# Turning half of x2 on VectorE and by transfers instead of TensorE, in a fused attention and feed-forward kernel

## The chip, the cores and the metric

The kernel runs on one core of one Trainium2 chip. The metric is device time in microseconds (us). A profile of one execution stands beside the times.

## What is computed

Inputs are x (32 batches, 32 steps, 512 features, float32), a condition index and a length per batch, and the weights of one layer. Cut to what matters:

```python
h = einsum('bct,bcd->bdt', x, cond_w[cond_idx])        # mix of the 32 steps, per batch
q, k = rms_norm(h @ Wq + bq, gq), rms_norm(h @ Wk + bk, gk)   # 4096 wide
v = h @ Wv + bv                                        # 32 heads of 128
x2 = x + softmax(q k^T / sqrt(128)) v @ Wo + bo
K = kernel(log_dt, C, log_A_real, A_imag, 512)         # 32 channels, 512 taps
y = causal_conv(x2, K) + x2 * D                        # along the 512 features
y = y * (arange(512) < length[batch])
out = x2 + y @ ffn_w + ffn_b + lora(y, gate, lora_a, lora_b) + shared_lora(y)
```

The step axis of x2 (32) is the channel axis of the convolution, and its feature axis (512) is the time along which the convolution runs.

## The kernel before

All engines have an instruction stream written out by hand, with semaphores between them. Tokens are (batch, step) pairs, 1024 of them, in G = 8 groups of P = 128 tokens: group g holds batches 4g to 4g + 3 (BPG = 4), each with 32 steps. Features are cut into KC = 4 chunks of 128. TensorE's products are split in three (high times high, high times low, low times high), so one product of 128 contraction rows is three matmuls.

The stages, in order: the mix; q, k and the scores for 32 heads; the values; then eight attention units (UNITS), each of one group of eight heads (OCT) and one half of the tokens (HG = 4 groups). A unit n has attend(n), 64 matmuls into the banks of PV_BANK; ACT's attn_out(n), which evicts them into at_hi; DVE's, which makes at_lo; then project_first(n) and project_second(n, g), which multiply by Wo into O_BANK; and DVE's accumulate(n, ...), which adds each of the four groups to acc. acc starts as x + bo and is x2 at the end. Unit 6 is the last for groups 0 to 3, unit 7 for groups 4 to 7. acc_ok counts DVE's additions.

The convolution wants x2 with the features on the partitions. So transpose_x2(g) (L1113) turns one group on PE, four transposes of 128x128 into a bank, and ACT's x2_out(g) (L1481) evicts the bank into x2p, laid out [feature, step, chunk, batch]. In unit 7, groups 0 to 3 are turned between project_first and project_second, groups 4 and 5 between the projections, and 6 and 7 after them. Then come five small matmuls (spin, L1165), whose result isn't used, and convolve(0). convolve(u) (L1137) does four channels, one in each 32-column quadrant of PE: for each chunk, x2p as the stationary operand (32 batches) and a Toeplitz view of the kernel (toep0 for u < 4, toep1 then) as the moving one. DVE masks the result (y_tok), PE turns it back (turn), ACT writes y_hi and y_t, DVE y_lo. The low-rank products and the feed-forward follow, and DVE adds acc to each group of the output (L1923).

DMA: SP's queue issues nearly all transfers in one order. In unit 7 these are ffn_raw (L450), toep0 (L453, 4 MB), sixteen small transfers of a_turn (L456) and four of b_turn (L458) to DRAM, all in pieces of 128 B, and, once these have landed, a_all, b_all and fb_rows. a_turn and b_turn are the low-rank weights turned by DVE in 32x32 blocks (L1877, L1878). POOL adds the feed-forward's bias (fb_rows) to acc, group by group (L795), and DVE waits for that before it adds acc to the output. ACT's own queue is used only for a few small loads at the start.

The addresses of several tiles overlap in time: x2p has the place of p_blocks, the attention weights of the unit being computed.

## Time and profile before

| | us |
|---|---|
| three runs | 806.17, 805.47, 806.24 |
| median | 806.17 |
| the profiled execution | 805.49 |
| its span in the profile | 803.7 |

The granted TensorE clock is 1.0 in the whole span. Busy shares of the span: PE 99%, PE's weight loads 81%, DVE 80%, POOL 65%, ACT 41%. The page also gives the chain of waits that ended last, the costliest groups of instructions and the transfers. All moments below are in us from the start of the span.

### The profile page before, as it was taken

The numbers are of one execution on the slowest core, as the hardware profiler recorded it, in microseconds if no ns is written. First come the engines' busy times: TensorE is split into PE (matmuls) and PEld (weight loads), VectorE is DVE, ScalarE is ACT, GpSimd is POOL, SyncE is SP. The second block draws the span as 40 slices with busy tenths as digits, with TensorE's granted clock in tenths as the row PEclk, the third lists the DMA queues.
The fourth block names the chain that finished last, engine by engine and source line by source line (L and its number), as shares of the span: only waits on it lengthen the run. The fifth ranks groups of instructions, "written<-read, shape, count | busy, mean of one in ns | idle before, by whom it ended". The sixth has DMA issues, their size and how long they took to land.

```text
span 803.7 us, 15196 instructions
## 1 busy us (share of the span) xinstructions
PE 795.6 (99%) x6093; PEld 651.7 (81%) x6093; DVE 643.1 (80%) x646; ACT 332.2 (41%) x374; POOL 520.5 (65%) x451
## 2 busy tenths in 40 slices
PE   9999999999999999999999999999999999999998
PEld 7777888888888888888888888888888888888466
DVE  7799888888888888987889769989899888861442
ACT  4655555555555555572222226322422331322520
POOL 4999887333333333428998995979999999910420
PEclk9999999999999999999999999999999999999999
DMA  7031111111111111304434421456404813418502
GB/s 207 28 85 50 52 52 52 53 52 52 52 52 52 52 52 42 115 2 157 182 139 180 180 105 55 169 79 187 157 1 157 316 61 147 157 50 257 127 18 88
DMA packets 80735, 81.87 MB, mean 102 GB/s; under 512 B 26044, under 2 KB 61212, under 8 KB 78652
## 3 DMA queue, kind: packets, MB, share of 16 engines
q1 hardware_dynamic: 80188, 81.24, 31.2%
q8 instruction: 25, 0.41, 0.2%
q10 hardware_dynamic: 512, 0.13, 0.1%
q14 instruction: 10, 0.08, 0.0%
HBM read 64.97 MB, written 16.40 MB: 101 GB/s over the span
## 4 chain that ended last, share of the span: by engine, by line
PE 91%; DVE 3%; POOL 3%; ACT 2%; DMA 1%; issue 1%; SPq 0%; DVEq 0%; POOLq 0%
PE psum L862 13%; PE psum L864 12%; PE psum L863 12%; PE psum L808 7%; PE psum L810 7%; PE psum L809 7%; PE psum L1061 7%; PE psum L1090 4%; PE psum L1092 4%; PE psum L1091 4%; PE psum L1078 3%; PE psum L1080 3%; PE psum L1079 3%; PE psum L901 3%; PE psum L1149 1%; DMA w_raw<-in_wk 1%
## 5 line engine op out<-in xcount | busy, mean ns | idle before, releaser
L506 POOL TENSOR_TENSOR w_raw<-w_raw 128x256 f32<-128x256 f32 x31 | 45.1, 1454 | 123.1 <-DMA w_raw<-in_wk 122.6
L862 PE MATMUL psum<-t_hi,w_hi 128*128 128x512 f32 x248 | 100.5, 405 | 0.0
L864 PE MATMUL psum<-t_hi,w_lo 128*128 128x512 f32 x248 | 96.5, 389 | 0.0
L863 PE MATMUL psum<-t_lo,w_hi 128*128 128x512 f32 x248 | 96.5, 389 | 0.0
L1370 ACT ACTIVATE sq<-qk_sb 128x1024 f32<-128x1024 f32 x31 | 32.9, 1063 | 140.7 <-issue 127.5
L1637 DVE TENSOR_TENSOR sumsq<-sumsq,sq 128x1024 f32<-128x1024 f32 x62 | 80.2, 1295 | 0.0
L1409 ACT ACTIVATE at_hi<-psum,params 128x512 fp32r<-128x512 f32 x64 | 44.0, 688 | 69.6 <-PE psum L1061 69.6
L862 PE MATMUL psum<-mix_hi,w_hi 128*128 128x512 f32 x186 | 72.5, 390 | 0.2 <-DVE w_lo L1541 0.2
L863 PE MATMUL psum<-mix_lo,w_hi 128*128 128x512 f32 x186 | 72.4, 389 | 0.0
L864 PE MATMUL psum<-mix_hi,w_lo 128*128 128x512 f32 x186 | 72.4, 389 | 0.0
L1541 DVE TENSOR_TENSOR w_lo<-w_raw,w_hi 128x1792 fp32r<-128x1792 f32 x30 | 61.4, 2047 | 1.5 <-ACT w_hi L1246 1.5
L1061 PEld LDWEIGHTS psum<-p_blocks,v_sb 128*128 128x128 f32 x512 | 58.5, 192 | 0.7
L1061 PE MATMUL psum<-p_blocks,v_sb 128*128 128x128 f32 x512 | 58.6, 275 | 0.0
L1826 DVE SCALAR_TENSOR_TENSOR at_lo<-psum,params,at_hi 128x512 fp32r<-128x512 f32 x64 | 47.2, 748 | 11.4 <-ACT at_hi L1409 5.0
L862 PEld LDWEIGHTS psum<-t_hi,w_hi 128*128 128x128 f32 x248 | 46.5, 187 | 10.6 <-DVE qk_sb L1629 1.1
L864 PEld LDWEIGHTS psum<-t_hi,w_lo 128*128 128x128 f32 x248 | 46.5, 188 | 10.1
L863 PEld LDWEIGHTS psum<-t_lo,w_hi 128*128 128x128 f32 x248 | 46.6, 188 | 8.3
L1246 ACT ACTIVATE w_hi<-w_raw 128x1792 fp32r<-128x1792 f32 (+2 forms) x32 | 52.8, 1651 | 1.1 <-POOL w_raw L511 1.0
L1078 PE MATMUL psum<-wo_hi_a,at_hi 128*128 128x512 f32 x128 | 50.5, 395 | 1.0 <-DVE wo_lo_a L1796 1.0
L1090 PE MATMUL psum<-wo_hi_b,at_hi 128*128 128x512 f32 x128 | 50.3, 393 | 0.1
L1080 PE MATMUL psum<-wo_hi_a,at_lo 128*128 128x512 f32 x128 | 49.9, 389 | 0.0
L1092 PE MATMUL psum<-wo_hi_b,at_lo 128*128 128x512 f32 x128 | 49.8, 389 | 0.0
(287 smaller groups left out, 2130.2 us busy)
## 6 DMA issues: line engine op xcount, KB each, us to landing
v_sb<-v_scr_dram SPq DMA_DIRECT2D x6, 2048.0 KB, 7.9
v_scr_dram<-v_sb SPq DMA_DIRECT2D x9, 1024.0 KB, 3.9
w_raw<-in_wq SPq DMA_DIRECT2D x32, 256.0 KB, 2.9
w_raw<-in_wk SPq DMA_DIRECT2D x32, 256.0 KB, 3.2
wv_raw<-in_wv SPq DMA_DIRECT2D x16, 512.0 KB, 4.4
toep<-kpad_dram SPq DMA_DIRECT2D x2, 4096.0 KB, 14.5
wo_raw_a<-in_wo SPq DMA_DIRECT2D x4, 1024.0 KB, 5.2
wo_raw_b<-in_wo SPq DMA_DIRECT2D x4, 1024.0 KB, 5.2
```

Source lines behind the costliest of these rows:

```text
L808: mm(out, lh, rh, start=(fresh and n == 0), stop=False)
L809: mm(out, lh, rl, start=False, stop=False)
L862: mm(bank(n), wh, hi[:, c, tok], start=(i == 0), stop=False)
L863: mm(bank(n), wh, lo[:, c, tok], start=False, stop=False)
L864: last = mm(bank(n), wl, hi[:, c, tok], start=False, stop=(i == 1))
L1061: last = mm(bank(PV_BANK[u % 4])[:, P * g:P * g + P], v_sb[:, part, g, cols], p_blocks[:, u, g, :], start=True, stop=True)
L1078: mm(bank(O_BANK[g]), at_hi[:, h, tok], wo_hi_a[:, h, :], start=(h == 0), stop=False)
L1080: last = mm(bank(O_BANK[g]), at_lo[:, h, tok], wo_hi_a[:, h, :], start=False, stop=False)
L1090: mm(bank(O_BANK[g]), at_hi[:, QUAD + h, tok], wo_hi_b[:, h, :], start=False, stop=False)
L1092: last = mm(bank(O_BANK[g]), at_lo[:, QUAD + h, tok], wo_hi_b[:, h, :], start=False, stop=(h == QUAD - 1))
L1541: v.tensor_tensor(w_lo[slot][:].rearrange("p b n -> p (b n)"), w_raw[slot][:, 1:8, :].rearrange("p b n -> p (b n)"), w_hi[slot][:].rearran ...
L1637: v.tensor_tensor(sumsq[:, m, :], sumsq[:, m, :], sq[:, m, :], ALU.add).then_inc(total, 1)
```

## The change

Four things are changed together.

1. The groups stand on the token axis in the order 0, 2, 4, 6, 1, 3, 5, 7 (GROUP_AT): position 0 to 3 hold the even groups, and are the half that unit 6 completes. The loads of x into x_nat and acc fetch the rows in that order, mix_w is indexed by it, and the output's addition looks the position up.
2. Positions 0 to 3 are no longer turned on PE. After a_turn and b_turn, DVE turns each of them in 32x32 blocks into x2_turn. ACT issues sixteen transfers, one for each quadrant of 32 partitions that the data leave and each that they reach, from x2_turn to x2p, and convolve(0) waits for all (x2_moved).
3. x2p is laid out [feature, chunk, group, batch in the group, step]. ACT's evictions write 128 elements in a row; the convolution's stationary operand takes every 32nd element.
4. The last group (position 7) is added, turned and evicted in two halves of 256 features, the second half through another bank. Two small matmuls stand before the convolution, not five.

x2_turn has the place of the tiles sm_s, turns and prod, whose last use is the softmax of unit 7. In the diff, declarations of semaphores and of tiles that only move are left out.

```diff
@@ -46,6 +46,7 @@
 O_BANK = (0, 1, 6, 7)
 OUT_BANK = (6, 7, 4, 5)
 GROUP_ORDER = (3, 0, 1, 2)
+GROUP_AT = (0, 2, 4, 6, 1, 3, 5, 7)
 UNITS = ((3, 1), (3, 0), (0, 0), (0, 1), (1, 0), (1, 1), (2, 0), (2, 1))
 HG = G // 2
 NCOND, NLORA, RANK = 16, 16, 32
@@ -148,12 +149,13 @@
             [("mix_f", [P, KC, TOK], F32)],
             [("wv_raw", [P, 4, 2, 512], F32)],
             [("p_blocks", [P, OCT, HG, P], F32)],
-            [("x2p", [P, SEQ, KC, BATCH], F32)])
-
-        (las_nat, las_t, lbs_nat, lbs_t, kzero), (sm_s, turns, prod), (y_tok, o_stage) = overlay(
+            [("x2p", [P, KC, G, BPG, SEQ], F32)])
+
+        (las_nat, las_t, lbs_nat, lbs_t, kzero), (sm_s, turns, prod), (x2_turn,), (y_tok, o_stage) = overlay(
             [("las_nat", [P, KC, 32], F32), ("las_t", [P, KC, RANK], F32),
              ("lbs_nat", [P, KC, RANK], F32), ("lbs_t", [P, KC, 32], F32), ("kzero", [32, P], F32)],
             [("sm_s", [P, OCT, HG, 32], F32), ("turns", [P, 16, 32], F32), ("prod", [P, 16, 32], F32)],
+            [("x2_turn", [P, KC, KC, HG, SEQ], F32)],
             [("y_tok", [P, 2, FEAT], F32), ("o_stage", [P, 2, FEAT], F32)])
         u_tab = prod
         k_sb = turns[:, 0:8, :]
@@ -312,7 +315,7 @@
         @block.sync
         def _(sp):
             def load_x(n):
-                sp.dma_start(x_nat[:, 2 * n:2 * n + 2, :], x_rows[:, 2 * n:2 * n + 2, :]).then_inc(x_in[n], 16)
+                sp.dma_start(x_nat[:, 2 * n:2 * n + 2, :], x_rows[:, GROUP_AT[2 * n]:GROUP_AT[2 * n] + 3:2, :]).then_inc(x_in[n], 16)
             for n in range(2):
                 sp.dma_start(cond_nat[NCOND * n:NCOND * n + NCOND], cond_w.rearrange("n c d -> n (c d)")).then_inc(cond_in, 16)
@@ -411,7 +414,7 @@
             sp.dma_start(bo_rows, every_partition(bo, FEAT)).then_inc(bo_in, 16)
             sp.wait_ge(vp_mm, 2 * 28)
             for half in (1, 0):
-                sp.dma_start(acc[:, HG * half:HG * half + HG, :], x_rows[:, HG * half:HG * half + HG, :]).then_inc(acc_in[half], 16)
+                sp.dma_start(acc[:, HG * half:HG * half + HG, :], x_rows[:, half:G:2, :]).then_inc(acc_in[half], 16)
             for done in (vq1_out, vq2_out, vk2_out):
@@ -791,7 +794,10 @@
             gp.tensor_scalar(mask[:], mask[:], len_col[:, 0:1], None, ALU.is_lt).then_inc(mask_ok, 1)
             pool.wait_ge(bias_in, 16)
             for g in range(G):
-                pool.wait_ge(xt_mm, g + 1)
+                if g < HG:
+                    pool.wait_ge(x2_turned, g + 1)
+                else:
+                    pool.wait_ge(xt_mm, g - 3 if g < 7 else 5)
                 gp.tensor_tensor(acc[:, g, :], acc[:, g, :], fb_rows[:], ALU.add).then_inc(bias_ok, 1)
@@ -837,7 +843,7 @@
                         pe.wait_ge(mixf_ok, 1)
                 for c in range(KC):
                     last = mm(bank(2 + n % 6)[:, P * c:P * c + P], x_nat[:, g, P * c:P * c + P],
-                              mix_w[:, g, :], start=True, stop=True)
+                              mix_w[:, GROUP_AT[g], :], start=True, stop=True)
                 last.then_inc(mix_mm, 1)
@@ -1110,28 +1116,31 @@
                     if n == 0 and g == 1:
                         kern()
-            def transpose_x2(g):
-
-                pe.wait_ge(acc_ok, HG * 6 + g + 1)
-                if g >= 4:
-                    pe.wait_ge(x2p_ok, g - 3)
-                for c in range(KC):
-                    last = nc.tensor.transpose(bank(PV_BANK[g % 4])[:, P * c:P * c + P], acc[:, g, P * c:P * c + P], ident[:, :])
+            def transpose_x2(g, part=range(KC), to=None):
+
+
+                for c in part:
+                    last = nc.tensor.transpose(bank(PV_BANK[g % 4] if to is None else to)[:, P * c:P * c + P], acc[:, g, P * c:P * c + P], ident[:, :])
                 last.then_inc(xt_mm, 1)
             attend(7)
             project_first(7)
             pe.wait_ge(alo_ok, OCT * 8)
-            for g in range(4):
-                transpose_x2(g)
             project_second(7, 0)
             project_second(7, 1)
+            pe.wait_ge(acc_ok, HG * 7 + 1)
             transpose_x2(4)
             project_second(7, 2)
+            pe.wait_ge(acc_ok, HG * 7 + 2)
             transpose_x2(5)
             project_second(7, 3)
+            pe.wait_ge(acc_ok, HG * 7 + 3)
             transpose_x2(6)
-            transpose_x2(7)
+            pe.wait_ge(acc_ok, HG * 7 + 4)
+            transpose_x2(7, range(0, 2))
+            pe.wait_ge(acc_ok, HG * 7 + 5)
+            pe.wait_ge(x2p_ok, 1)
+            transpose_x2(7, range(2, 4), PV_BANK[0])
             def convolve(u):
@@ -1146,7 +1155,7 @@
                 for c in range(KC):
                     for q in range(BPG):
                         ch = 4 * u + q
-                        last = mm(bank(2 + u % 2)[quadrant(q), P * c:FEAT], x2p[:, ch, c, :],
+                        last = mm(bank(2 + u % 2)[quadrant(q), P * c:FEAT], x2p[:, c, :, :, ch].rearrange("p g b -> p (g b)"),
                                   backwards(toep[:, ch % 16, P * c:FEAT]), start=(c == 0), stop=(c == KC - 1),
                                   tile_position=(0, 32 * q))
                 last.then_inc(conv_mm, 1)
@@ -1162,8 +1171,9 @@
                                                ident[:, :])
                 last.then_inc(turn_mm, 1)
-            spin(5, ident[:, :], 7)
-            pe.wait_ge(x2p_ok, G)
+            spin(2, ident[:, :], 7)
+            pe.wait_ge(x2_moved, 16 * BPG * KC)
+            pe.wait_ge(x2p_ok, HG + 1)
             convolve(0)
             for u in range(1, 8):
                 convolve(u)
@@ -1478,14 +1488,22 @@
                     exp_scores(n + 2)
-            def x2_out(g):
-
-                act.wait_ge(xt_mm, g + 1)
-                sc.activation(x2p[:, :, :, BPG * g:BPG * g + BPG].rearrange("p s c b -> p c b s"),
-                              bank(PV_BANK[g % 4]).rearrange("p (c b s) -> p c b s", c=KC, b=BPG), ACT.Copy).then_inc(x2p_ok, 1)
-
-            for g in range(G):
-                x2_out(g)
+            act.wait_ge(x2_turned, HG)
+            for b in range(BPG):
+                for k in range(KC):
+                    act.dma_start(x2p[quadrant(k)].rearrange("p c (g e) b s -> p e b (c g) s", e=2)[:, 0, b],
+                                  x2_turn[quadrant(b), k].rearrange("p c g s -> p (c g) s")).then_inc(x2_moved, 16)
+
+            def x2_out(n, g, part=slice(0, KC), at=None):
+
+                act.wait_ge(xt_mm, n)
+                sc.activation(x2p[:, part, GROUP_AT[g], :, :],
+                              bank(PV_BANK[g % 4] if at is None else at).rearrange("p (c b s) -> p c b s", c=KC, b=BPG)[:, part], ACT.Copy).then_inc(x2p_ok, 1)
+
+            for n in range(1, 4):
+                x2_out(n, n + 3)
+            x2_out(4, 7, slice(0, 2))
+            x2_out(5, 7, slice(2, 4), PV_BANK[0])
             act.wait_ge(ffn_in, 16)
             sc.activation(ffn_hi[:].rearrange("p c n -> p (c n)"), ffn_raw[:].rearrange("p c n -> p (c n)"),
                           ACT.Copy).then_inc(fhi_ok, 1)
@@ -1876,11 +1894,21 @@
                     dve.wait_ge(lora, 2 * (2 * NLORA - 1))
                     v.transpose(a_turn[:].rearrange("p g c r -> p (g c) r"), a_sum[:].rearrange("p g (c f) -> p (g c) f", f=32)).then_inc(turned, 1)
                     v.transpose(b_turn[:].rearrange("p g c o -> p (g c) o"), b_sum[:].rearrange("p g c r -> p (g c) r")).then_inc(turned, 1)
+                    dve.wait_ge(acc_ok, HG * 7)
+                    for g in range(HG):
+                        v.transpose(x2_turn[:, :, :, g, :].rearrange("p k c s -> p c k s"),
+                                    acc[:, g, :].rearrange("p (c k f) -> p c k f", c=KC, k=KC)).then_inc(x2_turned, 1)
                 accumulate(n, (0, 1))
                 if n % 2 == 1 and n < 7:
                     split_o(n // 2 + 1, 0)
-                accumulate(n, (2, 3))
-
+                accumulate(n, (2, 3) if n < 7 else (2,))
+
+            for half in range(2):
+                cols = slice(256 * half, 256 * half + 256)
+                if half == 0:
+                    dve.wait_ge(wo_mm, HG * 8)
+                    dve.wait_ge(acc_ok, HG * 6)
+                v.tensor_tensor(acc[:, 7, cols], bank(O_BANK[3])[:, cols], acc[:, 7, cols], ALU.add).then_inc(acc_ok, 1)
             dve.wait_ge(fhi_ok, 1)
             v.tensor_tensor(ffn_lo[:].rearrange("p c n -> p (c n)"), ffn_raw[:].rearrange("p c n -> p (c n)"),
@@ -1920,7 +1948,7 @@
                 dve.wait_ge(out_mm, g + 1)
                 if g >= 2:
                     dve.wait_ge(out_dma[g % 2], 16 * (g // 2))
-                v.tensor_tensor(o_stage[:, g % 2, :], bank(OUT_BANK[g % 4]), acc[:, g, :], ALU.add).then_inc(out_ok, 1)
+                v.tensor_tensor(o_stage[:, g % 2, :], bank(OUT_BANK[g % 4]), acc[:, GROUP_AT.index(g), :], ALU.add).then_inc(out_ok, 1)
 _INS = [("x", "x", (TOK, FEAT), F32), ("cond_idx", "itok_B_0_15", (BATCH,), I32),
```

What moves on PE: the end of attention and the start of the convolution. L1119 and, after, L1123 are the transposes of x2 (acc into a bank), L1090 to L1092 and L1096 to L1098 the last projections, L817 and L823 the spin, L1149 and L1158 the convolution. Before, between the two projections of unit 7:

```order
L1080 MATMUL psum<-wo_hi_a,at_lo 128x512
L1119 MATMUL psum<-ident,acc 128x128 [waits acc_ok,alo_ok]
L1119 MATMUL psum<-ident,acc 128x128 x3
L1119 MATMUL psum<-ident,acc 128x128 [waits acc_ok]
L1119 MATMUL psum<-ident,acc 128x128 x3
L1119 MATMUL psum<-ident,acc 128x128 [waits acc_ok]
L1119 MATMUL psum<-ident,acc 128x128 x3
L1119 MATMUL psum<-ident,acc 128x128 [waits acc_ok]
L1119 MATMUL psum<-ident,acc 128x128 x3
L1090 MATMUL psum<-wo_hi_b,at_hi 128x512 [waits alo_ok,wolo_ok]
```

These sixteen are gone after. The end of PE's part before, from the last projection on:

```order
L1092 MATMUL psum<-wo_hi_b,at_lo 128x512
L1119 MATMUL psum<-ident,acc 128x128 [waits x2p_ok,acc_ok]
L1119 MATMUL psum<-ident,acc 128x128 x3
L1119 MATMUL psum<-ident,acc 128x128 [waits x2p_ok,acc_ok]
L1119 MATMUL psum<-ident,acc 128x128 x3
L817 MATMUL psum<-ident 128x128 x5
L1149 MATMUL psum<-toep,x2p 32x512 [waits toep_in0,x2p_ok]
```

and the same place after:

```order
L1098 MATMUL psum<-wo_hi_b,at_lo 128x512
L1123 MATMUL psum<-ident,acc 128x128 [waits acc_ok]
L1123 MATMUL psum<-ident,acc 128x128 x3
L1123 MATMUL psum<-ident,acc 128x128 [waits acc_ok]
L1123 MATMUL psum<-ident,acc 128x128
L1123 MATMUL psum<-ident,acc 128x128 [waits x2p_ok,acc_ok]
L1123 MATMUL psum<-ident,acc 128x128
L823 MATMUL psum<-ident 128x128 x2
L1158 MATMUL psum<-toep,x2p 32x512 [waits toep_in0,x2p_ok,x2_moved]
```

The last group's transposes stand in two pairs with a wait each, and the convolution waits for the transfers too.

ACT after its last evictions of attention (L1409, after L1419), before:

```order
L1409 ACTIVATE at_hi<-psum,params 128x512 [waits pv_mm] x8
L1484 ACTIVATE x2p<-psum 128x4x4x32 [waits xt_mm] x8
L1490 ACTIVATE ffn_hi<-ffn_raw 128x2048 [waits ffn_in]
L1497 ACTIVATE y_hi<-psum 128x128x4 [waits turn_mm]
L1498 ACTIVATE y_t<-psum 128x128x4
```

and after (x_turn is x2_turn):

```order
L1419 ACTIVATE at_hi<-psum,params 128x512 [waits pv_mm] x8
L1494 DMA x2p<-x_turn 32x16x32 [waits x2_turned]
L1494 DMA x2p<-x_turn 32x16x32 x15
L1500 ACTIVATE x2p<-psum 128x4x128 [waits xt_mm] x3
L1500 ACTIVATE x2p<-psum 128x2x128 [waits xt_mm] x2
L1508 ACTIVATE ffn_hi<-ffn_raw 128x2048 [waits ffn_in]
```

Five evictions stand where there were eight, and sixteen issues ahead of them.

## Rows read from the trace of the kernel before

**Rows 1.** The page, chain that ended last, shares of the span by engine

```profile
PE 91%; DVE 3%; POOL 3%; ACT 2%; DMA 1%; issue 1%; SPq 0%; DVEq 0%; POOLq 0%
```

**Rows 2.** The chain in order of time: start us, us, what

```profile
730.12 1.75 PE psum L1119 x16
...
743.73 0.45 PE psum L1119 x4
744.20 2.07 ACT x2p L1484 x2
```

**Rows 3.** Timeline (start us, us, engine, line, operation [idle before]) and one line's durations (ns)

```profile
721.80 1.20 DVE L1878 STREAM_TRANSPOSE b_turn<-b_sum 128x1024 f32<-128x1024 f32 x1
734.64 0.69 DVE L1840 TENSOR_TENSOR acc<-psum,acc 128x512 f32<-128x512 f32 x1 [11.63 <-PE psum L1092]
...
746.33 4.51 PE L1149 MATMUL psum<-toep,x2p 128*32 128x512 f32 x64
...
L1484 ACT ACTIVATE x2p<-psum x8: 1062/1090/1130, 730.6 to 745.2; 128x512 f32<-128x512 f32 x8
```

**Rows 4.** One line's durations, ns min/median/max: ACT's mix_f from PSUM

```profile
L1255 ACT ACTIVATE mix_f<-psum x4: 597/598/598, 11.1 to 16.5; 128x512 f32<-128x512 f32 x4
```

**Rows 5.** SP's queue, 723 to 727 us, and a_turn's sixteen transfers

```profile
723.44 4.19 SPq L456 DMA_DIRECT2D a_scr_dram<-a_turn  x1
...
L456 SPq DMA_DIRECT2D a_scr_dram<-a_turn x16: 450/458/4189, 723.4 to 739.0; - x16
...
DMA to landing us min/median/max: 1.6/2.9/12.7
```

**Rows 6.** DMA traffic of 727 to 730, 730 to 735 and 735 to 737 us

```profile
DMA packets 582, 1.19 MB, mean 397 GB/s; under 512 B 0, under 2 KB 0, under 8 KB 582
...
DMA packets 950, 1.95 MB, mean 389 GB/s; under 512 B 0, under 2 KB 0, under 8 KB 950
...
GB/s 205 573 205 392 262 144 254 192 228 241 192 205 203 220 203 210 220 203 215 202 208 208 213 208 205 218 195 215 187 162 98 123 189 195 131 57 16 13 13 8
DMA packets 2506, 0.38 MB, mean 191 GB/s; under 512 B 2464, under 2 KB 2464, under 8 KB 2506
```

**Rows 7.** DMA traffic of 741 to 743 and 539 to 544 us; b_turn's issues

```profile
DMA packets 2091, 0.28 MB, mean 140 GB/s; under 512 B 2090, under 2 KB 2090, under 8 KB 2090
...
DMA packets 5611, 0.72 MB, mean 144 GB/s; under 512 B 5593, under 2 KB 5611, under 8 KB 5611
...
739.52 3.72 SPq L458 DMA_DIRECT2D b_scr_dram<-b_turn  x4
```

**Rows 8.** Transfers of ACT's queue at the start: KB each, us from issue to landing

```profile
cond_i<-in_cond_idx ACTq DMA_DIRECT2D x1, 2.0 KB, 2.1
...
prm_nat<-in_bv ACTq DMA_DIRECT2D x1, 16.0 KB, 5.6
```

**Rows 9.** b_all's transfers, and timeline of what waits for the loads

```profile
b_all<-b_scr_dram SPq DMA_DIRECT2D x2, 256.0 KB, 7.4
...
748.05 0.56 SPq L466 DMA_DIRECT2D b_all<-b_scr_dram  x1
...
761.26 1.91 ACT L1504 ACTIVATE b_hi<-b_all 128x2048 fp32r<-128x2048 f32 x1
...
756.67 12.01 POOL L795 TENSOR_TENSOR acc<-acc,fb_rows 128x512 f32<-128x512 f32 x8 [10.62 <-DMA fb_rows<-in_ffn_b]
```

**Rows 10.** Weight loads, ns min/median/max, and busy us of each engine in one stretch

```profile
L1101 PEld LDWEIGHTS psum<-expo,prod x64: 104/114/121, 531.2 to 532.1; 128*16 128x16 f32 x64
...
L1149 PEld LDWEIGHTS psum<-toep,x2p x256: 106/110/110, 746.3 to 767.9; 128*32 128x32 f32 x128
...
746.30:750.90 4.60, 4.51 (x64) 1.94 (x64) 2.89 (x2) 1.68 (x1) 0.00 (x0) 1.00 0.83 282
```

1 line of the change is left out of this document (added).

## The prediction

> **What bounds the kernel now.** I read the page's chain of waits first, then that chain in order of time near the end, then each engine's timeline there, then the DMA traffic. PE carries 91% of the chain that ended last [rows 1]. So a gain has to come off PE's own work or off the short stretch where the chain leaves it, and a change on any other engine counts only if PE comes to wait for it. The chain leaves PE for long where attention hands over to the convolution [rows 2]. At 730.12 it holds sixteen transposes of x2, 1.75 us for groups 0 to 3; later groups stand in it with 0.44 to 0.45 us each, the last but one at 743.73, right behind the last projection matmul. At 744.20 it moves to ACT, whose two evictions into x2p last until 746.27, and the first convolution matmul runs at 746.33 [rows 2, 3]. So the convolution starts 2.60 us after the last projection (743.73), and everything behind it (masks, turns, the low-rank part, eight output groups) hangs on it: a microsecond there is a microsecond at the end. I therefore only forecast when the convolution starts, against 746.33.
>
> **The change part by part.**
>
> *Sixteen PE transposes go.* They stand in the chain with 1.75 us [rows 2], and nothing takes their place: the projections that follow wait for at_lo, written long before. The last projection ends at 743.73 - 1.75 = 741.98.
>
> *The last group in halves, with the evictions contiguous.* Before, DVE adds the last group in 0.69 us, and ACT evicts groups 6 and 7 in 2.07 us, 1.06 to 1.13 us each, overlapping by 0.1 [rows 2, 3]. The new layout of x2p makes an eviction write runs of 128 elements in place of single elements 512 B apart; ACT's copies of that size from PSUM in contiguous runs take 0.60 us [rows 4], so half a group some 0.40 (half of 0.60 and a fixed 0.10, an estimate). With T for the last projection's end: the eviction of position 6 starts at T + 0.47 as now (744.20 - 743.73) and ends at T + 1.07; the first half's follows until T + 1.47; the second half's sum is ready at T + 0.04 + 0.82 (two halves of 0.69, each with some 0.06 more), its two transposes take 0.4, so its eviction runs to T + 1.87, and the convolution may start at T + 1.93. That is 0.67 us less than 2.60. Both gains together are 2.42 us: **if nothing else is late, the convolution starts at 743.9**.
>
> *Four VectorE transposes of 128x512.* DVE turns b_sum, twice that size, in 1.20 us, until 723.0, and then idles 11.6 us [rows 3]. So 0.6 each and 2.5 in all, done by 725.5, and hidden.
>
> *Sixteen transfers of 64 KB on ACT's queue.* Each is 32 partitions by 16 pieces of 128 B: 512 packets, 8192 in all, 512 on each of 16 DMA engines. ACT starts to issue at 725.6. The median issue of a_turn's transfers takes SP 0.46 us [rows 5], so ACT needs at least 7.4 us and is free by 733; its next work comes at 736, so this hides. Its cover is gone if the transfers' queue is full, as SP's is now: behind toep0 one issue took 4.19 us [rows 5]. ACT has then some 2.3 us of evictions to do (three at 0.5, two at 0.4) before 743.9, so it must be through its issues by 741.6.
>
> *What the transfers meet.* This term decides. At 723.03 SP issues toep0, 4 MB, and behind it 16 transfers of a_turn and 4 of b_turn, another 8192 packets of 128 B. Toep0's packets of 2 KB go at 950 in 5 us over 16 engines, 84 ns each on its engine [rows 6]. A packet of 128 B costs between 10 and 15 ns: 2464 in 2 us behind toep0 are 13.0 each, with 42 large ones among them, and that stretch's full slices, 203 to 220 GB/s, are 9.3 to 10; b_turn's 2090 in 2 us are 15.3; lb_nat's 5593 in 5 us, into SBUF, are 14.3 [rows 6, 7]. b_turn's four issues took 3.72 us [rows 7], 0.93 for 64 packets an engine, 14.5 ns a packet: there the issue set the pace. With work waiting in two queues an engine starves less, so I take 11 ns, near the slices of the backlog, and keep 10 and 14.5 for the range.
>
> How two queues share an engine no row shows for bulk traffic. The nearest are the small loads that ACT issues at the start beside SP's: the first lands in 2.1 us, the fifth of 16 KB, beside SP's full queue, in 5.6 [rows 8]. So ACT's queue has no precedence; its packets wait their turn. I take turns packet by packet. The first packets of x2 move at some 727. From there toep0 has 582 + 950 + 42 packets left [rows 6], 98 an engine. Beside each goes one of x2, which moves toep0's last, at some 735.3, by 98 x 0.013 to 736.6; x2 has then moved 98 of 512. The other 414 take turns with a_turn's and b_turn's (512 an engine, enough to last): 414 x 2 x 11 ns = 9.1 us, until 745.7. Landing adds about 1.0 (a_turn's shortest lands 1.6 us after its issue [rows 5], less the issue). **The transfers are complete at 746.7, and the convolution starts there, 0.4 us later than now.** The Trainium skill, DMA: Bandwidth & Descriptors, section Queues, rings and completion order, says that an engine goes round the queues that have work, one packet each, and that such a packet can hold several descriptors. How many these would hold no run here shows; filled by bytes and not by count, x2's turns would be through before 740 and the convolution would start at 743.9.
>
> *What is late next.* All DMA work now ends at about 748, some 4 us later, and SP, which waits for a_turn and b_turn to land before it loads a_all and b_all, resumes 4 us later. b_all's last transfer, issued at 748.05, lands after 7.4, at 755.5; 4 us later is 759.5, and ACT copies it at 761.3 [rows 9]. POOL's eight sums with fb_rows, 12.0 us from 756.7 [rows 9], would end at 773, before the last convolution's results have gone through the feed-forward. Both hide, b_all with 2 us to spare.
>
> *Edits at nothing.* The first loads and the acc load fetch the same rows in another order, in pieces of the same 2 KB. The three spin matmuls that go ran while PE waited for the eviction. The convolution's weight loads now step 128 B from element to element; loads of 16 columns at that step took 104 to 121 ns, while those of 32 adjacent columns take some 109 and are busy 1.94 of 4.60 us under the first two convolution units [rows 10], so even twice their time fits under the matmuls.
>
> **Sum.** 805.49 (the profiled execution; its span is 803.7) - 1.75 - 0.67 + 2.42 (both given back) + 0.4 = 805.9. The three runs' median is 806.17, 0.7 above that execution: forecast 806.6. A difference under 0.2%, 1.6 us, can't be told from none for this kernel.
>
> **The rivals.**
> 1. *Transfers in time.* If x2's packets go several to a turn, or ACT's queue gets half of the engines' time, they need 512 x 12 ns = 6 us of it, 12 at half share: through by 739, landed by 740. The convolution starts at 743.9, 2.4 us earlier: 803.8. For it: PE's and ACT's savings are certain. Against it: the load of ACT's queue that took 5.6 us beside SP's. The Trainium skill, same page, section Why small descriptors are slow (HBM only), says that SBUF to SBUF copies don't pay for small pieces, 128-byte packets reaching 78% of the link; no row here moves SBUF to SBUF. By that rule x2's packets cost about 6 ns (an estimate from that page's rate), the turns end at 743.6, and the gain is some 1.7 us. Chance 0.33.
> 2. *Forecast: late by about what was gained.* Turns packet by packet at 10 to 13 ns, landing between 744.7 and 747.9: 804.6 to 807.8. Chance 0.40.
> 3. *Slower: the transfers are the new wait.* The place is the wait for x2_moved before the first convolution; the price is x2's 414 remaining packets an engine. At 14.5 ns, b_turn's and lb_nat's rate, they last until 748.6 and land at 749.6: 3.3 us late, 809.4. It decides from a landing after 747.9, that is from 13 ns on, or from a start of x2's packets only once toep0 has left. For it: the rows of 14 to 15 ns are the long ones. If DMA work then lasts past 750, b_all comes after 761.3 too. Chance 0.22.
> 4. *The strided weight loads slow the convolution*, from three times their time on: four times 3 x 1.94 - 4.60, that is 4.9 us slower, 811. Against it: the loads of 16 columns. Chance 0.05.
>
> **The numbers.** Likeliest is 2: 806.6. Faster by over 1.6 us: 1, and 0.02 of 2: 0.35. Slower: 3 and 4, 0.27. Same: 0.38. The range takes in 1 with 0.5 us beyond it, and 3: 803.3 to 809.4; outside it are 4 and the tails.
>
> **What would show it.** In the profile after: sixteen transposes fewer on PE; evictions of 0.6 us where there were 1.09; DVE's four turns ending at 725.5; ACT's issues lasting 7.4 us, or far longer, and then the last eviction late. The release of PE's first convolution matmul tells the rest: ACT at 743.9 (rival 1), the transfers at 745 to 748 (2) or past 748 (3). Wrong would be: an x2 transfer that lands 2 us after its issue while toep0 runs; a convolution unit slower than before; ACT stalled on b_all.

## The result, and the profile after

| | before | after |
|---|---|---|
| median of 15 runs, us | 806.17 | 810.15 |
| lowest and highest | 805.38, 807.81 | 807.58, 814.28 |
| profiled execution | 805.49 | 809.73 |
| its span | 803.7 | 807.6 |

The ratio is 1.0053, 95% interval 1.0043 to 1.0064: the change makes the kernel slower by 0.5%, and the time lies 0.75 us above the forecast's range. None of the 15 executions of after has a mean granted clock above 0.998; of the 103 executions of the kernel before that ran beside the experiments, 76 have 1.000. One execution of the experiment with eight spins ahead of the transfers' wait took 1327.53 us at a mean granted clock of 0.557 and is left out of its median.

The chain of the page still belongs to PE (89%, [rows 1] 91%), but ACT's queue is in it now:

```profile
PE 89%; DVE 3%; POOL 3%; ACTq 2%; DMA 1%; ACT 1%; issue 0%; SPq 0%; POOLq 0%; DVEq 0%
```

The timeline of after at the handover (start us, us, engine, line, operation [idle before <- what ended it]) answers to [rows 3]:

```profile
724.39 2.45 DVE L1899 STREAM_TRANSPOSE x_turn<-acc 128x512 f32<-128x512 f32 x4
...
726.87 18.62 ACTq L1494 DMA_DIRECT2D x2p<-x_turn  x16
...
743.27 1.12 PE L1123 MATMUL psum<-ident,acc 128*128 128x128 f32 x6
...
744.24 4.07 SPq L461 DMA_DIRECT2D b_scr_dram<-b_turn  x4
745.54 2.13 ACT L1500 ACTIVATE x2p<-psum 128x512 f32<-128x512 f32 x5 [24.13 <-issue]
746.28 0.41 PE L1123 MATMUL psum<-ident,acc 128*128 128x128 f32 x2 [1.90 <-ACT x2p L1500]
746.53 0.61 PE L823 MATMUL psum<-ident 128*128 128x128 f32 x4
...
748.47 6.27 PE L1158 MATMUL psum<-toep,x2p 128*32 128x512 f32 x64 [1.33 <-DMA x2p<-x_turn]
```

VectorE's turns are as short and as early as forecast. ACT's sixteen issues are not: they last 18.6 us. ACT can therefore evict nothing before 745.54, PE stands idle 1.90 us for the bank, then 1.33 us for the transfers, and the first 64 convolution matmuls take 6.27 us where they took 4.51. The chain in order of time (start us, us, what) shows the same ([rows 2] of before):

```profile
744.14 0.66 ACTq L1494
...
744.84 3.59 DMA x2p<-x_turn
748.43 0.04 issue
748.47 6.27 PE psum L1158 x64
```

One tile's lines (ns min/median/max, first and last start) answer to [rows 3, 10]. Evictions take 0.60 us, forecast 0.60; weight loads went from 110 to 166 ns:

```profile
L1158 PEld LDWEIGHTS psum<-toep,x2p x256: 147/166/218, 748.5 to 772.0; 128*32 128x32 f32 x128
L1494 ACTq DMA_DIRECT2D x2p<-x_turn x16: 656/678/2920, 726.9 to 744.8; - x16
L1500 ACT ACTIVATE x2p<-psum x5: 403/592/603, 745.5 to 747.3; 128x512 f32<-128x512 f32 x3, 128x256 f32<-128x256 f32 x2
```

And busy time by stretch (stretch, length, busy us of PE, PEld, DVE, ACT, POOL with counts, granted clock, DMA share, GB/s), against a clock of 1.00 in [rows 10]: after PE's two idle waits the granted clock is at the lower level, 1.2 of 2.4 GHz, for 3.4 us of this stretch (3.8 us at a mean of 0.55).

```profile
748.40:752.20 3.80, 3.73 (x28) 1.41 (x32) 2.29 (x1) 1.07 (x1) 0.00 (x0) 0.55 0.66 96
752.20:757.00 4.80, 4.80 (x68) 2.95 (x64) 1.83 (x3) 1.09 (x2) 0.00 (x0) 1.00 0.91 298
```

The spans of the two profiled executions differ by 3.9 us (their times by 4.24, the rest lies outside the span). Counted between starts of PE instructions in both traces:

| from, to | before | after | difference |
|---|---|---|---|
| span's start to the 5000th matmul (far ahead of the change) | 631.96 | 633.42 | +1.46 |
| to the last projection | 111.38 | 109.61 | -1.77 |
| to the first convolution matmul | 2.99 | 5.44 | +2.45 |
| to the last one | 21.69 | 23.62 | +1.93 |
| to the last instruction | 35.63 | 35.45 | -0.18 |

### The profile page after: what moved, and what is told of

Same layout as the page of the kernel before. It is cut to its first block, busy times and chain, and to the rows that moved or that the text cites. A ratio compares the mean times of both kernels' runs of the same rounds, so it can differ in the third digit from the quotient of the medians.

```text
span 807.6 us, 15166 instructions
## 1 busy us (share of the span) xinstructions
PE 795.6 (99%) x6071; PEld 653.1 (81%) x6071; DVE 648.0 (80%) x651; ACT 325.9 (40%) x371; POOL 520.8 (64%) x451
## 4 chain that ended last, share of the span: by engine, by line
PE 89%; DVE 3%; POOL 3%; ACTq 2%; DMA 1%; ACT 1%; issue 0%; SPq 0%; POOLq 0%; DVEq 0%
PE psum L868 13%; PE psum L869 12%; PE psum L870 12%; PE psum L814 7%; PE psum L815 7%; PE psum L816 7%; PE psum L1067 7%; PE psum L1096 3%; PE psum L1097 3%; PE psum L1098 3%; PE psum L1084 3%; PE psum L1086 3%; PE psum L1085 3%; PE psum L907 3%; PE psum L1158 3%; ACTq L1494 2%
## 5 line engine op out<-in xcount | busy, mean ns | idle before, releaser
L1419 ACT ACTIVATE at_hi<-psum,params 128x512 fp32r<-128x512 f32 x64 | 44.0, 688 | 69.4 <-PE psum L1067 69.4
L1096 PE MATMUL psum<-wo_hi_b,at_hi 128*128 128x512 f32 x128 | 50.2, 393 | 0.4 <-DVE wo_lo_b L1814 0.4
L1097 PE MATMUL psum<-wo_lo_b,at_hi 128*128 128x512 f32 x128 | 49.9, 389 | 0.0
```

The source lines that it names most:

```text
L1096: mm(bank(O_BANK[g]), at_hi[:, QUAD + h, tok], wo_hi_b[:, h, :], start=False, stop=False)
L1097: mm(bank(O_BANK[g]), at_hi[:, QUAD + h, tok], wo_lo_b[:, h, :], start=False, stop=False)
```

## The experiments

"The wait" below is the time from the start of the last projection matmul to the first convolution matmul, 2.99 us before and 5.44 after. A ratio is always against the kernel before, run beside the experiment.

### Order of the groups alone

Against the kernel before; the acc load and the output's addition are indexed likewise.

```diff
+GROUP_AT = (0, 2, 4, 6, 1, 3, 5, 7)
-x_rows[:, 2 * n:2 * n + 2, :]
+x_rows[:, GROUP_AT[2 * n]:GROUP_AT[2 * n] + 3:2, :]
-mix_w[:, g, :], start=True
+mix_w[:, GROUP_AT[g], :], start=True
-x2p[:, :, :, BPG * g:BPG * g + BPG]
+x2p[:, :, :, BPG * GROUP_AT[g]:BPG * GROUP_AT[g] + BPG]
```

> The kernel before with the new order of the groups on the token axis alone: loads of x and acc, index of the mix weights, place of each eviction, lookup at the output. All eight groups are turned on TensorE as before. In the changed kernel's profile the first q and k products start 0.88 us later and everything after 1.1 to 1.5 us later, long before any edited stage. Theory O (the new order of the first loads costs it): 1.0 to 1.5 us slower than before, that is 807.2 to 807.7. Theory R (it is spread of that execution's start): within 0.4 us of before, and the first products at 17.0 us in the profile.

Measured: 806.71 us, ratio 1.0003 [0.9995, 1.0012]. Its own profiled execution reaches the 5000th matmul 0.58 us later than before's. The order costs nothing that can be measured. The 1.46 us in the first row of the table are spread of single executions: in the profiled executions of the nine experiments below that start from the changed kernel the same matmul comes from 0.7 us earlier to 0.8 us later than in before's.

### The new layout of x2p alone

Against the kernel before; ACT's evictions write the new layout.

```diff
-[("x2p", [P, SEQ, KC, BATCH], F32)]
+[("x2p", [P, KC, G, BPG, SEQ], F32)]
-x2p[:, ch, c, :]
+x2p[:, c, :, :, ch].rearrange("p g b -> p (g b)")
```

> The kernel before with x2p laid out feature, chunk, group, batch, step: evictions in contiguous runs, the convolution's weight loads at a step of 128 B. Theory W (strided weight loads slow the convolution, as the changed kernel's loads of 147 to 218 ns for 106 to 110 suggest): a convolution unit takes 2.35 us for 2.29, eight of them 0.5 us, against some 0.5 us gained at the last two evictions (1.09 to 0.6 each), so within 0.3 us of before. Theory C (those loads were slow only because the clock was low in the first two units): units of 2.29 us and 0.5 us faster than before.

Measured: 806.55 us, ratio 1.0003 [0.9994, 1.0011]. One tile's lines:

```profile
L1149 PEld LDWEIGHTS psum<-toep,x2p x256: 141/163/217, 747.0 to 768.8; 128*32 128x32 f32 x128
...
L1484 ACT ACTIVATE x2p<-psum x3: 597/597/599, 741.8 to 746.0; 128x512 f32<-128x512 f32 x3
```

The wait is 2.89 us in place of 2.99, since PE's own five spins now end later than the last eviction; but one convolution unit follows the next after 2.94 us where it was 2.88 (the kernel with the new order only). Seven such steps are 0.4 us. Gain and loss cancel: the strided weight loads are not free, though only 0.06 us of a unit's 32 loads shows.

### The change without its transfers

Against the changed kernel; GpSimd writes zeros in place of the even groups.

```diff
-            for b in range(BPG):
-                for k in range(KC):
-                    act.dma_start(
...
+            pool.wait_ge(pv_mm, OCT * 8)
+            gp.memset(x2p[:].rearrange("p c (g e) b s -> p e c g (b s)", e=2)[:, 0], 0.0).then_inc(x2_moved, 1)
...
-            pe.wait_ge(x2_moved, 16 * BPG * KC)
+            pe.wait_ge(x2_moved, 1)
```

> The changed kernel without the sixteen transfers; GpSimd fills the even groups' part of x2p with zeros once attention no longer reads that place, so the even groups' part of the convolution's input is left out. VectorE's turns stay. This is what the change would give if its transfers cost nothing. Theory T (the transfers carry the loss: late by some 4 us against what PE and ACT save, and the clock falls while PE waits): the convolution starts 2.4 us earlier than before relative to the last unit's start, granted clock 1.0 throughout, 804 to 805. Theory O (the loss is in the start of the kernel): that start stays 1.1 to 1.5 us late, 805 to 806. Rival S (strided loads and the shorter spin): above 806.

Measured: 804.36 us, ratio 0.9983 [0.9973, 0.9993]. The timeline of PE:

```profile
741.52 1.45 PE L1125 MATMUL psum<-ident,acc 128*128 128x128 f32 x8
742.80 0.61 PE L825 MATMUL psum<-ident 128*128 128x128 f32 x4
743.48 4.57 PE L1160 MATMUL psum<-toep,x2p 128*32 128x512 f32 x64
```

From the start of the last group's transposes to the convolution there are 1.96 us here. The prediction took its 2.60 and 1.93 us from the chain of waits, which puts the start of these transposes 0.16 us later than the timeline does. In this kernel's chain they start at

```profile
741.68 0.45 PE psum L1125 x4
```

so by the prediction's own clock 1.93 became 1.80. This is the change with transfers that cost nothing: 2.0 us faster. So the transfers cost the real change 5.8 us (810.15 - 804.36; the kernels before, run beside each, differ by 0.17).

### Eight spins in both of PE's waits

Against the changed kernel.

```diff
 transpose_x2(7, range(0, 2))
+spin(8, ident[:, :], 0)
...
-spin(2, ident[:, :], 7)
+spin(8, ident[:, :], 7)
 pe.wait_ge(x2_moved, 16 * BPG * KC)
```

> The changed kernel with eight small matmuls in place of none before the wait for the last two transposes, and eight in place of two before the wait for the transfers, so that TensorE is at work in the two gaps of 1.90 and 1.33 us of the changed kernel's profile. Theory P (the clock fell because PE stood idle): granted clock 1.0 in the stretch after, the first two convolution units take 4.6 us for 6.27, and the kernel is 1.7 us faster than the changed one, about 808.4. Theory D (the clock is chance, or the loss is the late transfers alone): 810 as the changed kernel, and the clock falls all the same.

Measured: 808.05 us, ratio 1.0018 [1.0008, 1.0027]; the convolution starts at 748.40, no earlier than in after, but at the full clock. The stretch that had a clock of 0.55 in after:

```profile
748.40:752.20 3.80, 3.80 (x53) 2.25 (x56) 2.70 (x2) 1.07 (x1) 0.00 (x0) 1.00 0.48 95
```

and its timeline:

```profile
748.40 4.58 PE L1159 MATMUL psum<-toep,x2p 128*32 128x512 f32 x64
```

Ten of its twelve executions have a mean clock of 1.000, of after's fifteen none. So the clock behind the idle waits, and not their length, costs 2.1 us of the 810.15 (2.3 if each is taken against its own kernel before): matmuls whose result nobody uses make the changed kernel faster by some 0.3%. The other 3.7 us between this kernel and the one without transfers (808.05 - 804.36) are lateness.

### Eight spins ahead of the transfers' wait only; five there

Against the changed kernel, twice: with eight as below, and with five, the number of before.

```diff
-spin(2, ident[:, :], 7)
+spin(8, ident[:, :], 7)
```

> The changed kernel with eight small matmuls in place of two before the wait for the transfers, and none before the last two transposes: PE still idles 1.9 us while it waits for ACT, but no longer 1.3 us behind that. Theory P2 (either gap alone is harmless): clock 1.0, as fast as with both gaps filled, 808.0. Theory P1 (the gap of 1.9 us is enough): the clock falls, 809.5 to 810.

> The changed kernel with five spin matmuls in place of two ahead of the convolution, as the kernel before had: the one part of the change that only shortened what TensorE does while it waits. Theory (the granted clock falls because TensorE idles 1.9 and 1.3 us in the 5 us ahead of the convolution): the second idle stretch shrinks to about 0.7 us, too little to matter if the first alone is enough for the fall: 809.5 to 810.2 with a granted clock of 0.5 for 3.4 us. Rival (the three removed spins tipped it): clock 1.0, first two convolution units in 4.5 us, 808.1, as with eight spins there.

Measured: 808.12 us, ratio 1.0034 [1.0020, 1.0049], and 808.35, ratio 1.0039 [1.0021, 1.0057]. Both profiled executions have a clock of 1.0, although PE idles longer there ahead of the last two transposes (2.39 and 2.59 us) than in after. With five spins:

```profile
746.27 0.41 PE L1123 MATMUL psum<-ident,acc 128*128 128x128 f32 x2 [2.59 <-ACT x2p L1500]
746.52 1.28 PE L823 MATMUL psum<-ident 128*128 128x128 f32 x10
748.32 4.57 PE L1158 MATMUL psum<-toep,x2p 128*32 128x512 f32 x64 [0.53 <-DMA x2p<-x_turn]
```

In this execution my theory for the five spins (809.5 to 810.2, clock 0.5 still) failed, and the rival's 808.1 is near. All executions together say less. With eight spins the profiled execution is the only one of seven at a mean clock of 1.000; the other six have 0.997 or 0.998. With five spins, five of ten have 1.000, three 0.998 and two 0.993, at 812.6 and 813.7. So spins ahead of the transfers' wait alone keep the clock up in some executions only, where spins in both waits did in ten of twelve: the idle time ahead of the last transposes counts too. What the removal of three spins costs is not shown. Against the kernel before on each occasion the medians give 1.4 and 1.6 us, but the intervals of both ratios overlap after's.

### SP held back until x2 has moved

Against the changed kernel, in SP's stream behind toep0.

```diff
+sp.wait_ge(x2_moved, 16 * BPG * KC)
```

> The changed kernel, but SyncE waits for the sixteen x2 transfers before it issues those of a_turn and b_turn, so that after toep0 nothing shares the DMA engines with x2. In the changed kernel x2's issues end 18.0 us after the first one starts, the last ten of them 0.66 to 0.69 us apart. Theory Q (the turns with a_turn's and b_turn's packets make x2 late): the last transfer lands some 4 us earlier, at 744 to 745, and the convolution's start is again set by ACT. Theory I (the issue of 512 small pieces takes ACT 0.66 us, whatever runs beside): the issues last as long as before after toep0 has gone, landing at 747 to 748. In both b_all comes later, and the kernel as a whole may be slower: only the start of the convolution is read.

Measured, one execution: 816.41 us. As said in the expectation, only the start of the convolution is read. ACT's queue and PE in the timeline:

```profile
724.74 18.32 ACTq L1495 DMA_DIRECT2D x2p<-x_turn  x16
...
745.33 6.27 PE L1159 MATMUL psum<-toep,x2p 128*32 128x512 f32 x64 [0.63 <-DMA x2p<-x_turn]
```

With no small packet of SP's in the way the issues last 18.3 us, against 18.6, and the convolution starts 20.6 us after the first of them, against 21.6 (22.1 in the execution with five spins, where the transfers also end the wait). So sharing the engines with a_turn and b_turn costs one or two microseconds; by the prediction's turns it would be half of 9.1. Theory I comes true: counted from after's first issue, this start would be at 747.5. Two things set the length: the fourth to the seventh issue take 1.1 to 2.7 us each while toep0 moves (the ninth 1.6, just behind it), and most later ones take 0.65 us each, which is what an issue of this size on ACT costs here. The first 64 convolution matmuls take 6.27 us as in after, behind idle waits of 1.60 and 0.63 us with two spins between. The 816.41 come from the rest: a_turn and b_turn are late by 8 us, ACT waits 7.2 us for b_all, PE idles, and the granted clock is 0.50 from 773.0 for 10.2 us.

### The turns and transfers eight microseconds earlier

Against the changed kernel: VectorE turns each group as soon as unit 6 has added it, no longer behind b_turn.

```diff
+                if n == 6:
+                    for g in range(HG):
+                        accumulate(6, (g,))
+                        dve.wait_ge(acc_ok, HG * 6 + g + 1)
+                        v.transpose(x2_turn[:, :, :, g, :].rearrange("p k c s -> p c k s"),
```

> The changed kernel with VectorE's four turns of x2 moved up, each right behind the last addition to its group in unit 6, into gaps of 1.2 to 2.0 us between those additions; ACT then issues the transfers at once after its last attention eviction, some 6 us sooner and ahead of toep0. Both theories of the transfers (turns shared, or issues of 0.66 us) say that they then land in time: five or six are through before toep0, the rest by 743 to 745. Then the convolution starts 1.3 to 2.4 us earlier than in the kernel before, the clock stays at 1.0, and the time is 804.5 to 806 (the strided weight loads take 0.4 of the gain back). Against it: if ACT's issues are held behind toep0 as in the changed kernel (2.6 to 2.9 us each), the landing moves by less than 3 us, and 807 to 808 comes out.

Measured: 807.43 us, ratio 1.0022 [1.0007, 1.0036]. The convolution starts at 743.99, with a wait of 3.11 us (2.19 without transfers), so most of their delay is gone. It is not all gone, since ACT's issues are held behind toep0 here too, the longest for 6.0 us. The kernel is still slower than before, outside the 804.5 to 806 that I expected and inside the 807 to 808 of the case against it, but for another cause: what is late next is b_all, and then PE:

```profile
760.68 1.94 ACT L1522 ACTIVATE b_hi<-b_all 128x2048 fp32r<-128x2048 f32 x1 [1.52 <-DMA b_all<-b_scr_dram]
```

The stretches of the same kernel:

```profile
769.50:776.30 6.80, 6.11 (x57) 5.72 (x57) 1.38 (x2) 1.28 (x3) 3.79 (x4) 0.50 0.01 2
```

ACT is held, so VectorE's b_lo, 2.95 us long and ahead of the mask of unit 6 in its order, ends only at 767.2. PE waits 1.64 us for that mask, until 767.9, and behind that the clock is at its lower level for 6.8 us. Seven of the ten executions have a mean clock of 0.998 or less; the median of the three at 1.000 is 805.79, against 805.59 for the kernel before.

### Pieces of 512 B instead of 128 B

Against the changed kernel. The batches stand in another order in x2p, so the lengths are loaded in it, and the turn of y_tok (last lines) puts them back.

```diff
-("x2p", [P, KC, G, BPG, SEQ], F32)
+("x2p", [P, KC, 2, BPG, HG, SEQ], F32)
-act.dma_start(x2p[quadrant(k)].rearrange("p c (g e) b s -> p e b (c g) s", e=2)[:, 0, b],
-              x2_turn[quadrant(b), k].rearrange("p c g s -> p (c g) s"))
+act.dma_start(x2p[quadrant(k), :, 0, b].rearrange("p c g s -> p c (g s)"),
+              x2_turn[quadrant(b), k].rearrange("p c g s -> p c (g s)"))
...
-ident[:, :])
+ident[:, :].rearrange("p (q j g) -> p q g j", q=4, g=HG))
```

> The changed kernel with x2p laid out so that one group of four pieces of 128 B lies in a row at both ends: each transfer is 128 pieces of 512 B and not 512 of 128 B. The batches then stand in another order in the convolution's rows; the lengths are loaded in that order, and the turn back to features puts them right with a permuted identity. Same bytes, same number of transfers, same moment of the first issue. Theory Q/I (the number of pieces makes the transfers late, by turns or by issue): landing before 741, convolution 2.1 to 2.4 us earlier than before as in the run without transfers, clock 1.0, 804.4 to 805. Rival B (bytes and the place behind toep0 make them late): little changes, above 808.

Measured: 806.25 us, ratio 1.0011 [1.0002, 1.0020]. The timeline of ACT's queue and of PE:

```profile
724.86 10.73 ACTq L1495 DMA_DIRECT2D x2p<-x_turn  x16
...
743.21 4.57 PE L1159 MATMUL psum<-toep,x2p 128*32 128x512 f32 x64
747.92 1.12 PE L1171 MATMUL psum<-ident,y_tok 128*128 128x128 f32 x4
```

With a quarter of the packets no issue is held: sixteen take 10.7 us, the convolution starts 2.2 us after the last projection, as without any transfer, and the clock stays at 1.0. The time is still above the 804.4 to 805 expected: the turn behind each unit takes 1.12 us where it took 0.66, eight times, since the identity is now read at a step of 16 B (the next experiment takes that away). An issue takes 0.63 us for 128 pieces, 0.66 for 512.

### The same with the reordered identity in a tile of its own

Against the kernel with 512 B pieces; VectorE writes the tile behind its turns of x2.

```diff
+turn_id = small[:, 0:4, :].rearrange("p a b -> p (a b)")
...
+v.tensor_copy(turn_id.rearrange("p (q g j) -> p q g j", q=4, g=HG),
+              ident[:, :].rearrange("p (q j g) -> p q g j", q=4, g=HG)).then_inc(turn_id_ok, 1)
...
-ident[:, :].rearrange("p (q j g) -> p q g j", q=4, g=HG))
+turn_id)
```

> The kernel with long pieces again (512 B, so 2048 packets in place of 8192), but the identity in the order of the new token axis stands in a tile of its own, written once by VectorE after the turns of x2, so that it is read in contiguous rows. Theory (the transposes behind each convolution unit took 1.12 us in place of 0.6 only since the identity was read at a step of 16 B): they take 0.6 us again, a unit and its turn are about as short as in the kernel without transfers (convolution span 22.1 us), the convolution starts right behind the last eviction, 2.2 us after the last projection (743.2 in the last run), the granted clock is 1.0, and the time is that of the kernel without transfers plus nothing: 804.3 +-0.6, ratio 0.998. Rival (the length of the pieces isn't what matters, or the order of the batches costs elsewhere): 806 or more. Second rival: b_all, issued some 2 us later than before, becomes the wait once the convolution is short: ACT's b_hi then stalls by more than 0.5 us and the time is near 805.5.

Measured: 807.20 us, ratio 1.0013 [0.9998, 1.0027]; five of twelve executions at a clock of 1.000 have a median of 805.33. The turns take 0.66 us again, so the step was the cause. The 804.3 expected was missed, and the second rival came true, first in the timeline, then in the stretches:

```profile
761.76 1.94 ACT L1526 ACTIVATE b_hi<-b_all 128x2048 fp32r<-128x2048 f32 x1 [2.15 <-DMA b_all<-b_scr_dram]
```

```profile
768.70:775.70 7.00, 5.94 (x44) 5.14 (x46) 2.82 (x5) 2.17 (x4) 5.67 (x5) 0.51 0.00 0
```

### Halves and layout, all groups on TensorE

The edit is shown against the kernel with the new layout alone; VectorE adds and ACT evicts the last group in halves too.

```diff
+            pe.wait_ge(acc_ok, HG * 8 + 1)
+            pe.wait_ge(x2p_ok, 5)
+            for c in range(2, KC):
+                last = nc.tensor.transpose(bank(PV_BANK[0])[:, P * c:P * c + P], acc[:, 7, P * c:P * c + P], ident[:, :])
...
-            spin(5, ident[:, :], 7)
-            pe.wait_ge(x2p_ok, G)
+            spin(2, ident[:, :], 7)
+            pe.wait_ge(x2p_ok, G + 1)
```

> The kernel before with the new layout of x2p and the last group in halves; all eight groups are turned on TensorE, nothing is transferred, the order of the groups is the old one. Forecast in the prediction for the halves with the contiguous evictions: 2.60 us from the last projection to the convolution become 1.93. The layout alone showed 2.89 against 2.99 (start to start) and gave 0.1. Theory: the halves bring that to about 2.2 to 2.4, the strided weight loads take 0.4 of it back, time 806.0 (+-0.5), so nearly all of what the kernel without transfers gained is the sixteen transposes. Rival: the halves are worth the 0.67 of the prediction or more, time 805.3 or less.

Measured: 805.86 us, ratio 1.0005 [0.9993, 1.0016]. From the start of the last group's transposes to the convolution it has 1.92 us in the timeline (745.29 to 747.21) and 1.76 us by the chain, for which the prediction had 1.93. So the halves and the contiguous evictions shorten this stretch by 0.84 us, not 0.67, but 0.47 us go again in the convolution, and nothing that can be measured is left. What the kernel without transfers gained is mostly the sixteen transposes.

### 512 B pieces and the identity's tile, with b_all's split later

Against the kernel with the identity in its own tile: ACT's b_hi two units later, VectorE's b_lo behind its last y_lo.

```diff
-                if u == 3:
+                if u == 5:
                     act.wait_ge(b_in, 64)
...
-                if u == 5:
-                    dve.wait_ge(bhi_ok, 1)
...
             y_low(7)
+            dve.wait_ge(bhi_ok, 1)
```

> The last kernel (long pieces, identity in the new order in its own tile) with ACT's split of b_all (b_hi) two convolution units later and VectorE's b_lo behind its last y_lo. In that kernel b_all, loaded some 3 us later than before, held ACT for 2.15 us at 761.8; the convolution's last results came late, TensorE waited 2.31 us at 769 and the granted clock was 0.5 for 6.8 us behind it in the profiled execution. Theory (both come from b_all): no wait of ACT on b_all, none of TensorE over 1 us between the convolution and the output, clock 1.0, and the time of the kernel without transfers, 804.3 +-0.6, ratio 0.998 against before. Rival (TensorE's wait at 769 had another cause, or another late transfer, fb_rows or a_all, takes over): 805.2 or more, as in the last kernel's executions of full clock.

Measured: **803.53 us**, ratio 0.9971 [0.9961, 0.9981], all eleven executions at a clock of 1.000 and between 803.1 and 804.5. It beats both kernels, and lies just below the 804.3 +-0.6 expected. Its timeline:

```profile
744.68 4.57 PE L1161 MATMUL psum<-toep,x2p 128*32 128x512 f32 x64 [0.23 <-ACT x2p L1504]
...
765.59 1.94 ACT L1526 ACTIVATE b_hi<-b_all 128x2048 fp32r<-128x2048 f32 x1
```

All of PE's waits from 740 us to the end (us in total, times, longest):

```profile
PE psum L1194 <- ACT y_t L1522: 0.8, 1, 0.8
PE psum L1161 <- ACT x2p L1504: 0.2, 1, 0.2
PE psum L1173 <- DVE y_tok L1936: 0.2, 1, 0.2
```

Since this edit also takes b_lo (3.4 us long here) out of the convolution, the 2.3 us against before are not those of x2's new way alone. Whether b_lo's new place alone would help the kernel before was not tried.

## Why the prediction was wrong, step by step

- **Transposes, 1.75 us:** 1.77 in the table. Right.
- **Halves, 1.93 us to the convolution:** 1.76 and 1.80 by the same clock, where nothing else is late. The mechanism was right, the gain 0.1 to 0.2 us larger.
- **VectorE's turns, 2.5 us, hidden:** right.
- **The transfers' landing, forecast 746.7:** the convolution started at 748.47, and less the 1.46 us by which this execution ran late, 747.0. In this execution the term was right by 0.3 us; in the one with five spins, counted from the last projection, it was off by 0.9. That is close, but partly for a wrong reason. "I take turns packet by packet" holds: from 731 to 737 us, while toep0 moves, ACT's queue (q10) gets 1016 packets beside 1025 of SP's (q1; packets, MB, share of 16 engines):

```profile
q1 hardware_dynamic: 1025, 2.10, 95.4%
q10 hardware_dynamic: 1016, 0.13, 14.9%
...
q10 hardware_dynamic: 4662, 0.58, 62.9%
q1 hardware_dynamic: 2866, 0.35, 38.7%
```

  By the Trainium skill (DMA: Bandwidth & Descriptors, section Queues, rings and completion order) an engine drains a packet of some 9 to 17 descriptors before it turns to the next queue. If the packets of both queues hold as many, the counts come out equal too, so these rows do not speak against the page; they speak against packets filled to equal bytes, by which the prediction has x2 through before 740. With pieces of 512 B beside SP's of 2 KB the counts are equal as well (128 and 128 from 734 to 735 us).

  Two things were different from the prediction. x2's first packets move only at 730.8, 4 us after the first issue. And behind toep0 there are two stages: from 738 to 740 the queues still take turns, at 9.5 to 9.7 ns a packet on its engine (11 was taken, and rival 1 worked out 6; x2 alone, with SP held back, moved 1447 in its fastest microsecond, 11.1 ns each), but from 740 on x2 moves 680 to 840 packets a microsecond and SP's queue 270 to 450 (the lower rows are 739 to 745 us, 777 and 478 on average). 777 a microsecond is 512 packets in 0.66 us, the length of one issue.

  The step "414 x 2 x 11 ns" named the wrong limit and hit its size. ACT's issue cost of 0.46 us, taken from SP's median, was 0.66, and five issues took 1.1 to 2.9 us each behind toep0, as one of SP's did in [rows 5]; the prediction named that case and did not put it into the sum. The bounds of rival 2 have a slip: 10 to 13 ns give, by the prediction's own sum, a landing between 745.9 and 748.4, not 744.7 and 747.9.
- **The failed step: "Edits at nothing", and with it PE's wait priced by its length alone.** The forecast for this execution was 805.9. To it come 1.5 us of spread ahead of the change, 0.3 of landing and 1.9 of the convolution's own length: 1.6 in its first two units, at the lower clock, and 0.4 from strided weight loads. "The three spin matmuls that go ran while PE waited": they were part of what kept PE busy. No row of before shows PE idle for longer than 0.7 us there, so what an idle TensorE costs afterwards had no row, and I left it out instead of bounding it. In the medians, each taken against its own kernel before, the forecast was +0.4 us and +4.0 came. Of the 3.6 between them the clock behind the idle waits is 2.3 (after less the kernel with eight spins in both), the transfers' lateness 0.9 (3.7 in place of 2.8), and the rest of the change 0.4 (-2.0 without transfers in place of -2.4, about the size of the strided weight loads). "Even twice their time fits under the matmuls" was wrong in small: 1.5 times cost 0.4 us. Which part of the clock's 2.3 us the missing spins carry, and which ACT's late evictions, stays open.
- **b_all, "2 us to spare":** less the late start its last issue came 3.6 us later, forecast 4. That was right, but it hid in after only because the convolution was late too. In the three kernels with transfers, an early convolution and b_hi in its old place ACT waited for it: 1.5 us, 0.4 (where the slow turns left it time) and 2.2.
- **The rivals:** rival 3 had the sign and the place, the wait for x2_moved, but its 809.4 came from a landing at 749.6; as before's clock reads it the landing was 747.0, and the rest of the loss is the clock's. That 810.15 lies near 809.4 is luck. Rival 1's 803.8 is about what the transfers would give in time: 804.36 without them, 803.53 with long pieces and b_all's split later. Rival 4's mechanism exists at a twelfth of its price.

## What to carry to other kernels

Price a wait of the busiest engine not by its length but by what stands behind it: here 3.2 us of idle TensorE cost about 2 us more in the granted clock, and unused matmuls placed in the wait bought them back. Before work is moved to a DMA queue, count pieces and issues: with the same bytes in a quarter of the packets the convolution started as early as without any transfer. And when a chain is shortened, look at the next thing that was nearly late; here b_all ate the gain twice before its place was changed.

## What the runs showed of the hardware

- ACT's issue of a 64 KB transfer took 0.62 to 0.68 us, whether of 128 or 512 pieces (the first of each sixteen 0.75); of the sixteen with 512 pieces, five took up to 2.9 us behind a 4 MB transfer of SP's queue, of those with 128 pieces none.
- Two queues with work got equal numbers of packets, whatever their size: 1016 of 128 B beside 1025 of 2 KB in 6 us.
- The granted clock was at 0.5 for 3.4 us after idle stretches of 1.90 and 1.33 us with 0.6 us of matmuls between, and at 1.0 after 2.59 and 0.53 us with 1.3 us between; around other waits of PE (2.31 and 1.64 us) it was low for 6.8 us. It was at 0.5 again after 1.60 and 0.63 us with 0.6 us between. In other executions of one and the same kernel it differed.
- Weight loads of 32 columns took 106 to 110 ns from adjacent elements and 141 to 218 ns at a step of 128 B (medians 110 and 163 to 166). Four 128x128 float32 transposes took 1.12 us with the moving operand at a step of 16 B, and 0.66 us from adjacent elements. The Trainium skill (SBUF — State Buffer, section Door 1: The DMA port swizzle) tells of 16-byte lines and of a stride that is free up to four float32; at a step of exactly four elements it was not free here, which fits what the same passage asks for, at least two accesses to each line.
